# Two routed adapter layers on one Trainium2 core: new order for the weight splits and for two steps of the row work

## The reference

```
h = gelu(x @ W_down + b_down)          # 1024 -> 512
y = x + h @ W_up + b_up                # 512 -> 1024
x = (y - mean(y)) / sqrt(var(y) + eps) * gain + beta
```

## Time and profile before

| | |
|---|---|
| median of three runs | 2749.48 us (2748.82 to 2749.53) |
| the profiled execution | 2748.52 us, of which the span from the first to the last instruction is 2746.7 us |
| busy: PE, weight load | 2686.8 us (98%), 2207.3 us (80%) |
| busy: DVE | 2209.5 us (80%) |
| busy: ACT, POOL | 1669.8 us (61%), 1388.9 us (51%) |
| mean granted TensorE clock | 0.992 |
| matmuls of the down product (L517) | 6240, 813.2 + 812.1 + 812.0 us busy |
| matmuls of the up product (L529) | 5460 |

### The profile page before, as it was taken

The page is one execution under the profiler, slowest core; times in us unless marked ns, Lnnn a source line. Parts: engine busy times, 40 slices in busy tenths (PEclk is TensorE's granted clock), DMA queues, the critical chain, the costliest instruction groups (busy, mean ns, idle before and its releaser), DMA issues.

```text
span 2746.7 us, 54496 instructions
## 1 busy us (share of the span) xinstructions
PE 2686.8 (98%) x11714; PEld 2207.3 (80%) x11714; DVE 2209.5 (80%) x3357; ACT 1669.8 (61%) x2905; POOL 1388.9 (51%) x1050
## 2 busy tenths in 40 slices
PE   8999999999999999999989999999989999999997
PEld 6888888887788888888768888888778888888885
DVE  6777777778777777777898888888888888888886
ACT  4666656666666665665656656665656566665664
POOL 1455555455555555555545454454444455545545
PEclk9999999999999999999999999999999999999998
DMA  6656656566665666656756566666756665666654
GB/s 224 211 193 215 212 199 213 203 230 227 216 215 201 206 209 205 214 199 225 243 185 223 193 215 213 196 212 206 250 184 216 200 223 195 217 204 203 216 190 149
DMA packets 360582, 573.29 MB, mean 209 GB/s; under 512 B 40144, under 2 KB 239952, under 8 KB 359248
## 3 DMA queue, kind: packets, MB, share of 16 engines
q1 hardware_dynamic: 358704, 554.14, 60.3%
q10 hardware_dynamic: 1440, 15.47, 1.5%
HBM read 364.97 MB, written 204.47 MB: 207 GB/s over the span
## 4 chain that ended last, share of the span: by engine, by line
PE 88%; DVE 6%; issue 4%; ACT 1%; DVEq 1%; POOL 0%; DMA 0%; ACTq 0%; POOLq 0%; SPq 0%
PE pD L517 47%; PE bX L529 23%; PE bZ L529 18%; DVE wul L863 1%; DVE xt L961 1%; DVE hl L943 1%; DVE xT L914 1%; DVE wdl L844 0%; DVE xt L953 0%; DVE xl L921 0%; DVE hT L928 0%; DVE xt L984 0%; ACT wdh L601 0%; ACT pC L705 0%; DMA xt<-in_itok 0%
## 5 line engine op out<-in xcount | busy, mean ns | idle before, releaser
L517 PE MATMUL pD<-wdh,xh 128*128 128x512 f32 x2080 | 813.2, 391 | 18.9 <-DVEq L905 18.9
L517 PE MATMUL pD<-wdl,xh 128*128 128x512 f32 x2080 | 812.1, 390 | 0.0
L517 PE MATMUL pD<-wdh,xl 128*128 128x512 f32 x2080 | 812.0, 390 | 0.0
L462 POOL TENSOR_TENSOR xt<-xt,cgb 128x1024 f32<-128x1024 f32 x258 | 629.1, 2439 | 348.7 <-ACT xt L713 348.7
L470 POOL TENSOR_TENSOR cs<-hT 128x256 f32<-128x256 f32 x130 | 154.0, 1185 | 907.4 <-DVE hT L928 907.4
L705 ACT ACTIVATE pC<-xt,nmean 128x512 f32<-128x512 f32 x520 | 358.9, 690 | 260.6 <-DVE nmean L969 251.6
L713 ACT ACTIVATE xt<-xt,rstd 128x1024 f32<-128x1024 f32 x258 | 296.5, 1149 | 319.3 <-POOL rstd L448 315.6
L517 PEld LDWEIGHTS pD<-wdh,xh 128*128 128x128 f32 x2080 | 392.2, 189 | 103.7 <-DVEq L905 16.5
L517 PEld LDWEIGHTS pD<-wdh,xl 128*128 128x128 f32 x2080 | 392.2, 189 | 82.0
L517 PEld LDWEIGHTS pD<-wdl,xh 128*128 128x128 f32 x2080 | 392.3, 189 | 81.5
L529 PE MATMUL bX<-wuh,hh 128*128 128x512 f32 x1040 | 408.4, 393 | 16.3 <-DVE xt L953 8.2
(11 more groups left out here) (106 smaller groups left out, 3819.7 us busy)
## 6 DMA issues: line engine op xcount, KB each, us to landing
xq<-in_xB SPq DMA_DIRECT2D x130, 512.0 KB, 3.5
htok<-hg SPq DMA_DIRECT2D x260, 256.0 KB, 2.8
hq<-htok SPq DMA_DIRECT2D x1040, 64.0 KB, 2.1
xt<-in_x SPq DMA_DIRECT2D x130, 512.0 KB, 4.1
mid<-xt SPq DMA_DIRECT2D x130, 512.0 KB, 3.6
xq<-mid SPq DMA_DIRECT2D x520, 128.0 KB, 3.1
xt<-mid SPq DMA_DIRECT2D x130, 512.0 KB, 4.1
out<-xt SPq DMA_DIRECT2D x128, 512.0 KB, 3.0
```

What stands on the lines that cost most here:

```text
L462: eng.tensor_tensor(xt[:, k, :], xt[:, k, :], cgb[:, 1, :], ALU.add).then_inc(s_o, 1)
L517: last = eng.matmul(pD[e][:, :], a[:, e, 128 * k:128 * k + 128], w[:, k, :], start=False, stop=(k == 7 and n == 2), skip_group_check=True)
```

## The change

1. `take_wd_1` on ACT moves from the start of step i to the end of step i - 1 (behind `high_h(w, 3)`), and `take_wd_0` ahead of `seed_x` and `seed_z`. On DVE `take_wd_1` moves ahead of the two transposes of h.
2. The wait for the down bias moves into `seed_d` (a wait in every step, on the count of loads begun).
3. Factor 4 (`b11 = t2 - b11`) is made in `take_wu_1`, behind the low parts of factors 2 and 3, not in `take_wu_0`.
4. `take_wu_2` on DVE splits only factor 4; a new `take_wu_3` splits 5 and 6. P4 waits for s_wu[2], P5 and P6 for s_wu[3].
5. In every step of DVE the fourth eviction (`last_onto(u, 4)`) comes ahead of `scale(u-1, 0)`, and `scale(u-1, 1)` behind the fifth eviction.

```diff
@@ -150,7 +150,7 @@
         s_wd = [sem(f"s_wd{k}") for k in range(2)]
         s_wuh = sem("s_wuh")
         s_wul = sem("s_wul")
-        s_wu = [sem(f"s_wu{k}") for k in range(3)]
+        s_wu = [sem(f"s_wu{k}") for k in range(4)]
         s_sub = sem("s_sub")
         s_xq = [sem(f"s_xq{k}") for k in range(2)]
         s_x = [sem(f"s_x{k}") for k in range(XB)]
@@ -523,7 +523,7 @@
 
             def product(u, n, left, bank, start=False):
                 if u.exists():
-                    count(eng, s_wu[min(n // 2, 2)], u, 1, 1)
+                    count(eng, s_wu[(0, 0, 1, 1, 2, 3, 3)[n]], u, 1, 1)
                     for c in range(2):
                         for m, (a, w) in enumerate(((hh, wuh), (hh, wul), (hl, wuh))):
                             last = eng.matmul(bank[:, :], a[:, left, 128 * c:128 * c + 128], w[:, n, c, :],
@@ -571,7 +571,7 @@
             fd = Phases(eng, "ac_fd", 1)
             fu = Phases(eng, "ac_fu", 1)
             pd = [Phases(eng, f"ac_pd{g}") for g in range(2)]
-            pb = Phases(eng, "ac_pb")
+            pb = Phases(eng, "ac_pb", 1)
             pg = [Phases(eng, f"ac_pu{g}") for g in range(2)]
 
             def adapter(p):
@@ -585,12 +585,9 @@
 
             def load_bias(p):
                 row = adapter(p)
+                pb.next()
                 count(eng, s_sd, p + -1, 2, 2)
                 eng.dma_start(cbd[:, :], bd[row, :].broadcast_to([128, K])).then_inc(s_bd, 16)
-
-            def bias_landed(p):
-                eng.wait_ge(s_bd, pb.next() * 16 + 16)
-                eng.sem_inc(s_seen, 1)
 
             def high_wd(p, c, q):
                 count(eng, s_Db, p + -1, 4, q + 1)
@@ -660,6 +657,8 @@
                 if p.exists():
                     if p.first():
                         eng.wait_ge(s_bits, 1)
+                    if e == 0:
+                        eng.wait_ge(s_bd, eng.snap(pb.reg) * 16)
                     count(eng, s_hg, p + -1, 2, e + 1)
                     eng.activation(pD[e][:, :], cbd[:, :], ACT.Copy).then_inc(s_sd, 1)
 
@@ -714,7 +713,6 @@
 
 
             high_x(Pair(0), 0)
-            bias_landed(Pair(0))
             seed_d(Pair(0), 0)
             take_wd_0(Pair(0))
             eng.wait_ge(s_ctl, 1)
@@ -722,7 +720,6 @@
 
             def begin(i):
                 kinds.read(i + 2)
-                kinds.when_new(i, take_wd_1)
                 high_x(i, 1)
                 gelu(i + -1, 1)
                 seed_d(i, 1)
@@ -750,16 +747,16 @@
                 gelu(i, 0)
                 high_h(w, 2)
                 if not (i + 1).first():
-                    kinds.when_new(i + 1, bias_landed)
                     seed_d(i + 1, 0)
                 normal(u + -1, 1)
+                if not (i + 1).first():
+                    kinds.when_new(i + 1, take_wd_0)
                 seed_x(w)
                 seed_z(w)
-                if not (i + 1).first():
-                    kinds.when_new(i + 1, take_wd_0)
                 square(u, 0, 0)
                 square(u, 0, 1)
                 high_h(w, 3)
+                kinds.when_new(i + 1, take_wd_1)
                 square(u, 1, 0)
                 square(u, 1, 1)
 
@@ -878,8 +875,6 @@
                 eng.tensor_tensor(cbu[:, K:H], cbu[:, K:H], cbu[:, 0:K], ALU.subtract).then_inc(s_bz, 1)
                 low_wu(c * 7, 0, b11)
                 low_wu(c * 7, 1, b12)
-                eng.wait_ge(s_wul, c * 7 + 1)
-                eng.tensor_tensor(b11, t2, b11, ALU.subtract).then_inc(s_sub, 1)
                 eng.wait_ge(s_wul, c * 7 + 2)
                 eng.sem_inc(s_seen, 1)
                 eng.wait_ge(s_bz, c + 1)
@@ -889,12 +884,18 @@
                 c = pg[1].next()
                 low_wu(c * 7, 2, t2)
                 low_wu(c * 7, 3, b22)
+                eng.wait_ge(s_wul, c * 7 + 1)
+                eng.tensor_tensor(b11, t2, b11, ALU.subtract).then_inc(s_sub, 1)
                 eng.wait_ge(s_wul, c * 7 + 4)
                 eng.sem_inc(s_seen, 1)
 
             def take_wu_2(p):
+                low_wu(eng.snap(pg[2].reg) * 7, 4, b11)
+                eng.wait_ge(s_wul, eng.snap(pg[2].reg) * 7 + 5)
+                eng.sem_inc(s_seen, 1)
+
+            def take_wu_3(p):
                 c = pg[2].next()
-                low_wu(c * 7, 4, b11)
                 low_wu(c * 7, 5, b21)
                 low_wu(c * 7, 6, t4)
                 eng.wait_ge(s_wul, c * 7 + 7)
@@ -1018,10 +1019,10 @@
                     last_rows(u + -1)
                     return
                 onto(u, 1, X, 0, 0)
+                kinds.when_new(i, take_wd_1)
+                ready(i, s_wd[1])
                 transpose_h(w, 0)
                 transpose_h(w, 1)
-                kinds.when_new(i, take_wd_1)
-                ready(i, s_wd[1])
                 low_x(i, 1)
                 kinds.read(i + 1)
                 onto(u, 2, bZ, 1, 1)
@@ -1031,16 +1032,18 @@
                 onto(u, 3, X, 0, 1)
                 kinds.when_new(u, take_wu_2)
                 ready(u, s_wu[2])
-                kinds.when_near(w, factors)
                 if not u.last():
                     variance(u + -1)
+                last_onto(u, 4, bZ, 0, 1, 3)
+                kinds.when_new(u, take_wu_3)
+                ready(u, s_wu[3])
+                kinds.when_near(w, factors)
                 if only_up(i):
                     low_h(w, 1)
                 scale(u + -1, 0)
-                scale(u + -1, 1)
-                last_onto(u, 4, bZ, 0, 1, 3)
                 transpose_x(i + 1, 0)
                 last_onto(u, 5, X, 1, 1, 2)
+                scale(u + -1, 1)
                 kinds.when_new(w, take_wu_0)
                 ready(w, s_cb)
                 ready(w, s_wu[0])
```

## The result

The changed kernel takes 2795.03 us (median of four runs, 2793.73 to 2796.41) against 2749.4 us of the kernel before on the same chip: ratio 1.0168, 95% interval 1.0155 to 1.0181. It is slower by about 46 us; the prediction had 25 slower and a range that ended at 2783. The profiled execution took 2796.41 us, with a span of 2794.6.

A forecast was written before the change was run, and what follows sets the result against it. PE, busy 98% of the span, was taken as the bound, so only its stops count. From the profiled 2748.52 us, + 18.4 + 3.6 - 4.2 + 6.8 + 1.8 - 1.2 = + 25.2 gave 2773.7, stated as 2774.5; range 2750 to 2783.

The forecast's parts named there:

- Part 1: Ordinary step of layer 1: POOL's shift 0 holds scale 1 for 1.95 us, mean at T + 18.4, no cost there.
- Part 2, layer 0: Loop turns of layer 0: PE starts at 26.3 for 25.84, 0.45 us late in eight turns, 3.6 us lost.
- I move it with the mean: Loop turns: the jump, with DVE's stand (4.49 or 4.06 us, 3.63 in layer 0), comes later together with the mean.
- Part 2, layer 1: Loop turns of layer 1: P2 2.5 us late in four turns and 2.1 in four, 18.4 us lost.
- The lag: Ordinary step of layer 1: DVE's second half runs 2.5 us later, or 0.6 if scale 1 isn't held.
- Part 3: First W_up: with the split, P4 starts when due and P5 at about 65.65; 4.2 us gained.
- Part 4: Three changes of adapter: 6.8 us later for the up weights and 1.8 later for the down weights.
- splitting the semaphore gives it back: Three changes of adapter: P5 comes 2.2 to 2.6 us earlier behind P2, against the lag of +2.3 to +2.7.
- Part 5: Last three steps: PE's wait of 3.16 us ahead of P5 is removed twice; 1.2 us gained.
- Scale 1 not held: Rival for the scales: the lag is only 0.6 us, sum - 4.7, 2744.8 us; chance 0.15.
- Turns unpaid: Rival at the loop turns: the stand starts before the mean, so the lag costs nothing there, 2752.7 us; chance 0.09.
- PE's clock halved at the turns: Rival: stops in eight turns also halve PE's clock, 1.7 us each, 13.6 in all, 2788 us; chance 0.06.

The follow-up runs named there:

- short shift: Changed kernel, but POOL's shift adds the last term to 64 of the 1024 columns only: 2728.85 us, ratio 0.9922.
- early ready: Changed kernel, but without a new adapter next, DVE counts s_wd[0] up right behind the mean, ahead of the loop jump: 2790.56 us, ratio 1.0148.
- scales together: Changed kernel with scale 1 right behind scale 0 again, both behind the moved fourth eviction: 2762.66 us, ratio 1.0048.
- twelve steps: Changed kernel with DVE's loop twelve steps long in place of six, the other engines keeping six: 2769.97 us, ratio 1.0079.

## Why the prediction was wrong

- **Part 1 held to a tenth.** Scale 1 waits for the shift, the mean comes at T + 18.34, and in an ordinary step nothing is lost. The Trainium skill, "GPSIMD Engine Reference", Key points, says that Vector instructions with two SBUF inputs contend with GpSimd. The 3.14 us of the scale here agrees with it, and the short shift is the test.
- **Part 2, layer 0, failed** (3.6 predicted, 11.8 measured): the step "I move it with the mean", that is, the stand keeps its length. It was read as a property of the jump, 3.63 us, and was 4.40. The load of xq had come 0.76 us behind the mean and now comes 0.37 ahead of it. In SP's queue it follows the first store by 2.33 us, before and changed, and that store waits for shift 0; it came only 1.16 us later in the step, the mean 2.31:

```profile
560.34 0.36 SPq L365 DMA_DIRECT2D mid<-xt  x1
562.66 0.35 SPq L318 DMA_DIRECT2D xq<-in_xB  x1
...
562.57 0.36 SPq L365 DMA_DIRECT2D mid<-xt  x1
564.90 0.35 SPq L318 DMA_DIRECT2D xq<-in_xB  x1
```

  The first two rows are from before (T = 545.86), the others changed (T = 546.93). The first eviction then comes at T + 26.23 and not T + 25.5, and PE's P2 at T + 27.04 for the 26.3 predicted. That is 1.2 us lost in place of 0.45. Most of what is left of a turn's 1.5 comes at P3, which starts 0.08 us late and whose second matmul follows after 0.34 us and not 0.23, as it does behind every stop.
- **Part 2, layer 1, was 5.1 us low** (18.4, 23.5), by the same step. The stands there were 4.54 us in the mean of eight (4.30 before, by the same eight), which is 1.9 us in eight turns, and the pause ahead of `low_h(w, 3)` was 0.31 us longer, 2.5 in eight. The lag itself came out a little under its term. With that P2 is 21.8 us late in eight turns; the other 1.7 is behind P2, in the pitch behind the stops. The gate at D00 was missed, but it is not a cause: see early ready.
- **Part 3 held** (4.2, 3.9 measured). The granted clock (third from the end) of the stretch that had 0.91 in the earlier trace rows:

```profile
55.00:75.00 20.00, 19.95 (x88) 16.01 (x87) 16.40 (x28) 12.52 (x22) 4.84 (x4) 1.00 0.72 234
```

- **Part 4 was the other large miss** (8.6, 18.0). With the scales together the changes cost 6.2, so the hold costs 11.8 of it. Two terms failed. The first is the netting "splitting the semaphore gives it back". In change 2 the hold adds to P2 in step 67 (before, scales together, changed) and then, in step 69, where neither of the other two stops, to P0 and P2 (changed):

```profile
1383.69 0.50 PE L529 MATMUL bX<-wuh,hh 128*128 128x512 f32 x1 [0.36 <-DVE xt L953]
...
1383.26 0.50 PE L529 MATMUL bX<-wuh,hh 128*128 128x512 f32 x1 [1.00 <-DVE xt L954]
...
1400.79 0.50 PE L529 MATMUL bX<-wuh,hh 128*128 128x512 f32 x1 [2.61 <-DVE xt L954]
...
1448.28 0.47 PE L529 MATMUL bX<-wuh,hh 128*128 128x512 f32 x1 [0.46 <-issue]
1455.49 0.50 PE L529 MATMUL bX<-wuh,hh 128*128 128x512 f32 x1 [1.49 <-DVE xt L954]
```

  The split did remove the stops ahead of P4 and P5 in step 68 (2.15 and 0.81 us before), but P2 of that step grew from 1.65 to 2.70. Over the three changes PE's stops are 13.6 us longer, where the prediction had 8.6 in all. The second term was put at nothing: the slow clock behind the stops. Counted as in the last section, it adds 10.7 us in the changes for 7.1 before, 3.6 more.

  A gate was missed too. P0 waits for ACT's `seed_x`, which waits for DVE's count s_cb behind `take_wu_0`:

```profile
1419.57 0.60 ACT L671 ACTIVATE bX<-cbu 128x512 f32<-128x512 f32 x1 [4.25 <-DVEq L906]
...
1420.22 0.50 PE L529 MATMUL bX<-wuh,hh 128*128 128x512 f32 x1 [2.57 <-ACT bX L671]
```

  With the same at change 3 these are the two waits of 5.0 us in PE's list. But they are no part of the hold, for scales together has them with 5.0 us as well, and hardly a cost: they stand in for D00, which waited 2.80 us at 1403.46 before and 0.34 at 1422.25 changed. Which work of DVE makes each of the longer stops isn't taken apart further.
- **Part 5's sum held** (1.2, 1.9), with luck: PE's stops at the end are 8.1 us for 8.6, and the slow clock behind them went from 4.1 us to 0.1, which the prediction did not have. The last P0 comes 4.5 us earlier for it, and what follows takes 2.5 longer.
- **The rivals.** Scale 1 not held: refuted (3.14 us). Turns unpaid: refuted by twelve steps. PE's clock halved at the turns: refuted; none of the sixteen turns has a matmul at the slow pitch, and over the turn shown the granted clock is 1.00, the column behind PE's, DVE's, ACT's and POOL's busy time:

```profile
2218.00:2232.00 14.00, 11.24 (x49) 8.53 (x47) 8.07 (x15) 7.12 (x15) 3.85 (x4) 1.00 0.34 109
```

- **The range** ended at 2783. In the span the miss is 22.7 us, the sum of three terms with one sign (8.2, 5.1 and 9.4); the start and the end are off by 0.7 each way and cancel. All three are costs of a late DVE that I took from the kernel before with its stands, its pauses and PE's clock, as if only the mean moved.

## What to carry to other kernels

When an engine is made late, list every semaphore that it counts up behind the late point, also those that cost nothing today, and what it releases on the DMA queue: here the stand at the loop's jump was longer when a load came ahead of it, and moving that load gave 17 us back. An elementwise instruction on VectorE with two full SBUF inputs must not be put where GpSimd runs a long one; the place decides, not the amount of work. And a reorder that helps at four places should be made at those four, not in each of 130 steps.

## What the runs showed of the hardware that I had not expected

- The stand of DVE at a loop's jump isn't a constant. In layer 0 it was 3.1 to 3.3 us with no load near it (there ACT ended it; 3.6 once), 3.6 with one issued 0.8 us behind the mean (4.4 once, in early ready), and 4.1 to 5.1 with one issued just ahead of it (6.7 once, in the short shift near 440).
- POOL's shifts cost the kernel before time too. With 64 columns in place of 1024, and DVE in the poorer order, the kernel is 20.5 us (0.8%) faster than before; about 4 of these are the first W_up's.
- PE's clock did fall at some stops of the changes, not at others of the same length (none behind 2.55 us at 2047.12). Behind the stop of 2.61 us at 1400.79 the matmuls follow each other after 0.43 us and not 0.23 from 1401.47 to 1404.45, and over that stretch the granted clock is 0.53, that is, nearly all of it at the lower of the two levels (1.2 GHz, where 1.00 is 2.4):

```profile
1401.40:1404.80 3.40, 3.40 (x10) 2.64 (x9) 3.40 (x5) 1.05 (x2) 2.70 (x4) 0.53 0.47 145
```

  Such stretches (matmuls that start 0.36 to 0.47 us after the one ahead, less 0.227 each, from step 4 on) add 11.2 us in the kernel before and 10.8 in the changed one. So the clock has no part in the sum of 46 us, but it has moved: 3.6 us more in the changes, 4.0 less at the end.
